# A four-layer cross-attention network on one core: earlier keys in layer 0, two score buffers in layer 3, another maximum, earlier weights and an fp32 first product in the last network, a bf16 bias in layer 2

## What is computed

```
x = x + L0_xattn(layernorm(x), ctx, ctx)      # 16 heads of 8, linear attention over 64 positions
x = x + L0_ffn(...) ; x = x + L1_xattn(...) ; x = x + L1_ffn(...) ; x = x + L2_xattn(...)
# L2_ffn: top-1 of 8 experts with a capacity, and a residual MLP beside them
a   = layer_norm(x) * attn_nw + attn_nb
res = gelu(a @ res_inter_w + res_inter_b) @ res_output_w + res_output_b
x   = x + res * coef0 + moe * coef1
# L3_xattn: rotary positions, a mask of at most 5 keys for each query
keep   = (key <= seg_id) & (key >= seg_id - 4)
scores = where(keep, q @ k.T / sqrt(8), -inf)  # 64 x 64 for each of 16 heads and 128 sequences
x = x + softmax(scores) @ v @ Wo
# L3_ffn: 16-bit activations with one scale for the whole tensor, 8-bit weights
quantize_a16(x): s = 32767 / max|x| over all tokens and features; round(x * s) / s
quantize_w8(w):  s = 127 / max|w| along one axis;                 round(w * s) / s
hidden = gelu(quantize_a16(layernorm(x)) @ quantize_w8(W_in) + b_in)
x = x + quantize_a16(hidden) @ quantize_w8(W_out) + b_out
```

## Time and profile before

| | us |
|---|---|
| median of three runs | 3071.56 |
| the three runs | 3076.02, 3067.39, 3071.56 |
| time of the profiled execution | 3070.32 |
| its span (first to last instruction) | 3068.8 |
| TensorE (PE) busy in it | 2563.7 (84%) |
| VectorE (DVE) busy | 2210.2 (72%) |
| ScalarE (ACT) busy | 1393.5 (45%) |
| GpSimd (POOL) busy | 385.9 (13%) |
| mean granted clock of TensorE | 0.927 of full |

### The profile page before, as it was taken

The page is one execution under the profiler, slowest core; times in us unless marked ns, Lnnn a source line. Parts: engine busy times, 40 slices in busy tenths (PEclk is TensorE's granted clock), DMA queues, the critical chain, the costliest instruction groups (busy, mean ns, idle before and its releaser), DMA issues. The chain is left out here.

```text
span 3068.8 us, 68519 instructions
## 1 busy us (share of the span) xinstructions
PE 2563.7 (84%) x25419; PEld 1890.9 (62%) x25454; DVE 2210.2 (72%) x5434; ACT 1393.5 (45%) x2483; POOL 385.9 (13%) x542
## 2 busy tenths in 40 slices
PE   4867769995899999999999789887979786787457
PEld 3644436663887877878876466665657454666227
DVE  6889859996567767777775388896830486888784
ACT  3548868884011111111111477764534345666364
POOL 0012210000000000000000000002321442232004
PEclk9988779997999999999999799998989898999689
DMA  3110000002113112112120000001013220000001
GB/s 92 31 67 1 0 19 16 14 13 91 76 56 111 56 61 106 56 67 99 56 80 31 21 15 15 10 2 36 26 36 110 79 66 3 0 0 0 8 0 55
DMA packets 55450, 128.94 MB, mean 42 GB/s; under 512 B 9702, under 2 KB 21350, under 8 KB 54507
## 3 DMA queue, kind: packets, MB, share of 16 engines
q1 hardware_dynamic: 47754, 106.36, 10.0%
q0 software_dynamic: 7520, 20.34, 2.2%
HBM read 109.37 MB, written 17.30 MB: 41 GB/s over the span
## 5 line engine op out<-in xcount | busy, mean ns | idle before, releaser
L1505 PE MATMUL banks<-l1f_feed,l1f_w 128*128 128x512 f32 x512 | 229.1, 598 | 1.4 <-DVE l1f_feed L1774 1.4
L1448 PE MATMUL banks<-l1f_sums,l1f_mixes 128*128 128x256 f32 x768 | 186.6, 379 | 0.0
L1774 DVE TENSOR_TENSOR l1f_feed<-l1f_aoT,l1f_rwb 128x512 f32<-128x512 f32 x256 | 158.8, 682 | 15.8 <-PE banks L1448 10.3
L1505 PEld LDWEIGHTS banks<-l1f_feed,l1f_w 128*128 128x128 f32 x512 | 95.8, 192 | 108.5 <-issue 90.0
L1448 PEld LDWEIGHTS banks<-l1f_sums,l1f_mixes 128*128 128x128 f32 x768 | 145.9, 190 | 19.9
L1448 PE MATMUL banks<-l1f_feed,l1f_mixes 128*128 128x256 f32 x512 | 135.3, 387 | 20.5 <-DVE l1f_feed L1731 20.5
L1740 DVE TENSOR_TENSOR l1f_sums<-l1f_feed 128x512 f32<-128x512 f32 x128 | 88.5, 691 | 87.8 <-PE banks L1448 84.0
L1468 PE MATMUL banks<-l1f_w,l1f_feed 128*128 128x128 f32 x1024 | 136.7, 277 | 0.0
L214 POOL COPY x<-xn 128x512 f32 (+1 forms) x16 | 9.8, 611 | 935.6 <-DVE xn L1791 935.6
L1468 PEld LDWEIGHTS banks<-l1f_w,l1f_feed 128*128 128x128 f32 x1024 | 126.2, 194 | 0.0
L1448 PEld LDWEIGHTS banks<-l1f_feed,l1f_mixes 128*128 128x128 f32 x512 | 93.1, 192 | 38.7 <-DVE l1f_feed L1731 24.5
(11 more groups left out here) (524 smaller groups left out, 7057.5 us busy)
## 6 DMA issues: line engine op xcount, KB each, us to landing
l1f_rwb<-l1f_shares SPq DMA_DIRECT2D x128, 512.0 KB, 7.0
l0a_ctxT<-in_ctxT SPq DMA_DIRECT2D x16, 256.0 KB, 2.6
l2f_sent<-l0f_zero SPq DMA_DIRECT2D x4, 1024.0 KB, 7.0
l1a_ctxT<-in_ctxT SPq DMA_DIRECT2D x16, 256.0 KB, 2.6
l2c_ctxT<-in_ctxT SPq DMA_DIRECT2D x16, 256.0 KB, 2.7
l2e_rows<-l2f_sent SPq DMA_DIRECT2D x16, 256.0 KB, 2.8
l2f_answers<-l2e_y POOLq DMA_DIRECT2D x16, 256.0 KB, 2.7
l3p_ctxT<-in_ctxT SPq DMA_DIRECT2D x16, 256.0 KB, 2.6
```

What stands on the lines that cost most here:

```text
L1448: return pe.matmul(prods[:, n, :], left, right, start=(p == 0 and first), stop=(p == PAIRS - 1), skip_group_check=True)
L1505: pe.matmul(out_bank, w[:, 1, e, :], feed[:, e % NB, :], start=(e == 0), stop=(e == E - 1)).then_inc(s.y_psum, 1)
L1774: dve.tensor_tensor(feed[:, e % NB, :], aoT[:, m, :], rwb[:, m, e, :], ALU.mult).then_inc(s.ae_ready, 1)
```

## The change

Six edits.

1. Layer-0 attention: `keys` stands first in PE's list, before `turn`.
2. Layer-3 attention: the scores have two buffers, of two whole PSUM banks each (banks 0, 1 and banks 2, 3). `score` of tile t waits for `centred` of tile t-2. The mask is two matmuls of 512 columns in place of four of 256, the scores four matmuls on 64 rows and 512 columns in place of eight on 32 rows and 256 columns. For this POOL's `kbd` has 1024 columns in place of 512, and is made before the mask. All later parts run one step later.
3. Scales: DVE takes maximum and minimum of the first 24 tiles only. For the other 40, ACT writes the absolute distance from the mean, |mean - x|, and DVE takes one maximum for every 8 tiles of these. The weights are gone from this stage.
4. Up: ACT copies the turned activations once as fp32, and PE multiplies once in fp32; DVE's `lower` is gone, `win` is fp32.
5. Layer-2 experts: SP loads the last network's weights ahead of the first rows, DVE rounds them ahead of its bias pipeline, PE and ACT turn and copy the first matrix at the stage's end. Their buffers are allocated once for layers 2 and 3.
6. Layer-2 gate: the residual bias is a bf16 matmul of 96 rows, as in layer 0; DVE prepares its three parts after the weights' arrival.

```diff
-            pipeline(pe, k.NG, [(1, turn), (2, outer), (3, project), (1, keys), (1, queries), (2, weigh), (1, values), (2, turn_o)])
+            pipeline(pe, k.NG, [(1, keys), (1, turn), (2, outer), (3, project), (1, queries), (2, weigh), (1, values), (2, turn_o)])
...
-        scores = k.banks[:, 0:4, 0:4 * S].rearrange("p a (b n) -> p a b n", n=S)
+        scores = [k.banks[:, 2 * par:2 * par + 2, :].rearrange("p a (h n) -> p (a h) n", n=S) for par in range(2)]
...
-                if mask:
-                    mask.make(pool, t, par, s.score_psum)
                 wait(pool, s.score_psum, t - 1)
                 settle(pool, k)
-                pool.tensor_tensor(kbd[:, par],
-                                   r.kT[:, bass.ds(P * t, P)].rearrange("p (b n) -> p b n", b=2).unsqueeze(2).to_broadcast([P, 2, 4, S]),
-                                   k.headmask.unsqueeze(1).unsqueeze(3).to_broadcast([P, 2, 4, S]), ALU.mult).then_inc(s.q_ready, 1)
+                pool.tensor_tensor(kbd[:, par], r.kT[:, bass.ds(P * t, P)].unsqueeze(1).to_broadcast([P, H // 2, P]),
+                                   k.headmask8.unsqueeze(2).to_broadcast([P, H // 2, P]), ALU.mult).then_inc(s.q_ready, 1)
+                mask.make(pool, t, par, s.score_psum)
...
-                wait(pe, s.centred, t)
-                    for a in range(4):
-                        pe.matmul(scores[:, a], never[:, :], rhs, start=True, stop=False, skip_group_check=True)
-                for a in range(4):
-                    lo = 32 * a
+                wait(pe, s.centred, t - 1)
+                for a in range(2):
+                    pe.matmul(ps[2 * par + a], never[:, :], rhs, start=True, stop=False, skip_group_check=True)
+                for a in range(2):
+                    rows = slice(64 * a, 64 * a + 64)
                     for b in range(2):
...
-            pipeline(pool, k.NT, [(5, copy_mv), (2, add_bias), (0, prepare)], unroll=TG)
+            pipeline(pool, k.NT, [(6, copy_mv), (2, add_bias), (0, prepare)], unroll=TG)
-            pipeline(pe, k.NT, [(1, score), (2, turn), (4, project), (3, weigh)], unroll=TG)
+            pipeline(pe, k.NT, [(2, score), (3, turn), (5, project), (4, weigh)], unroll=TG)
-            pipeline(act, k.NT, [(0, copy_q), (2, copy_v), (2, copy_pT), (1, exp)], unroll=TG)
+            pipeline(act, k.NT, [(0, copy_q), (3, copy_v), (3, copy_pT), (2, exp)], unroll=TG)
-            pipeline(dve, k.NT, [(1, centre), (3, normalise), (4, new_x)], unroll=TG)
+            pipeline(dve, k.NT, [(2, centre), (4, normalise), (5, new_x)], unroll=TG)
...
+            for t in range(FAR):
+                last = act.activation(away[:, t, :], k.x[:, OWN + t, :], ACT.Abs, bias=k.mv[:, OWN + t, 0:1], scale=-1.0)
...
-            for n in range(PIECES):
-                dve.tensor_reduce(ends[:, 0, piece], k.x[:, piece, :], AX_X, ALU.max).then_inc(s.ends_chain, 1)
-                dve.tensor_reduce(ends[:, 1, piece], k.x[:, piece, :], AX_X, ALU.min).then_inc(s.ends_chain, 1)
+            dve.tensor_reduce(ends[:, 0, :], k.x[:, 0:OWN, :], AX_X, ALU.max).then_inc(s.ends_chain, 1)
+            dve.tensor_reduce(ends[:, 1, :], k.x[:, 0:OWN, :], AX_X, ALU.min).then_inc(s.ends_chain, 1)
...
+            for n in range(FAR // PIECE):
+                dve.wait_ge(s.away_ready, n + 1)
+                dve.tensor_reduce(far[:, piece], away[:, piece, :], AX_X, ALU.max).then_inc(s.ends_chain, 1)
...
-                    pe.matmul(ps[4 + c], w.win[:, c, :], high[:, m, :], start=True, stop=False)
-                    pe.matmul(ps[4 + c], w.win[:, c, :], low[:, m, :], start=False, stop=True).then_inc(s.f_psum, 1)
+                    pe.matmul(ps[4 + c], w.win[:, c, :], hT[:, m, :], start=True, stop=True).then_inc(s.f_psum, 1)
...
-            pipeline(dve, k.NG, [(1, lower), (0, quantise), (2, largest)])
+            pipeline(dve, k.NG, [(0, quantise), (2, largest)])
...
-                pe.matmul(y_bank, k.ones[0:1, 0:P], b2[:, :], start=True, stop=False, skip_group_check=True)
+                pe.matmul(y_bank, ones[0:96, :], b2_rows[:, :].unsqueeze(1).to_broadcast([96, TG, D]), start=True, stop=False,
...
+            round_network()
             pipeline(dve, items, [(2, bias)], unroll=2 * per)
```

More of the change, by code:

```diff
@@ L2387, in _ @@
-            dve.wait_ge(s.rstd_ready, 1)
-            dve.tensor_tensor(ends[:, :, :], ends[:, :, :], both(k.rstd[:, :]), ALU.mult).then_inc(s.ends_chain, 1)
-            dve.wait_ge(s.ends_chain, 2 * PIECES + 2)
-            dve.tensor_reduce(w.most[:, 0:1], ends[:, :, :].rearrange("p a t -> p (a t)"), AX_X, ALU.max,
-                              apply_absolute_value=True).then_inc(s.most_ready, 1)
-            chain = Chain(dve, s.w_chain)
-            go = lambda ins: chain.wait(chain.did(ins))
@@ new lines, in _ @@
+            dve.wait_ge(s.ends_chain, 3 + FAR // PIECE)
+            dve.wait_ge(s.rstd_ready, 1)
+            dve.tensor_tensor(peaks[:, 0:2 * OWN].rearrange("p (a t) -> p a t", a=2), ends[:, :, :], both(k.rstd[:, 0:OWN]), ALU.mult)\
+                .then_inc(s.ends_chain, 1)
+            dve.tensor_tensor(peaks[:, 2 * OWN:], far[:, :], k.rstd[:, OWN:], ALU.mult).then_inc(s.ends_chain, 1)
+            dve.wait_ge(s.ends_chain, 5 + FAR // PIECE)
+            dve.tensor_reduce(w.most[:, 0:1], peaks[:, :], AX_X, ALU.max, apply_absolute_value=True).then_inc(s.most_ready, 1)
@@ L2415, in l3_ffn_up @@
+def l3_ffn_up(nc, k, w, hidden):
     FC = F0 // P
@@ L2459, in gelu @@
                     settle(act, k)
-                    act.activation(w.hidden[:, c, bass.ds(GT * g, GT)], ps[4 + c], ACT.Gelu,
+                    act.activation(hidden[:, c, bass.ds(GT * g, GT)], ps[4 + c], ACT.Gelu,
                                    bias=w.b_in[:, c:c + 1], scale=w.scale[:, 0, c:c + 1]).then_inc(s.f_ready, 1)
-            pipeline(act, k.NG, [(1, gelu), (0, split)])
+            pipeline(act, k.NG, [(1, gelu), (0, copy_hT)])
         @block.gpsimd
@@ L2768, in _ @@
             dve.wait_ge(s.weights, 16 * 7)
+            chain.did(dve.memset(b2_rows[:, :], 0.0))
+            go(dve.tensor_copy(b2_part[:, 0, :], b2[:, :]))
+            go(dve.tensor_tensor(b2_rest[:, :], b2[:, :], b2_part[:, 0, :], ALU.subtract))
+            go(dve.tensor_copy(b2_part[:, 1, :], b2_rest[:, :]))
+            go(dve.tensor_tensor(b2_rest[:, :], b2_rest[:, :], b2_part[:, 1, :], ALU.subtract))
+            go(dve.tensor_copy(b2_part[:, 2, :], b2_rest[:, :]))
+            for n in range(3):
+                last = dve.tensor_copy(b2_rows[32 * n:32 * n + 1, :], b2_part[32 * n:32 * n + 1, n, :])
+            last.then_inc(s.consts_ready, 1)
             def norm(g, m):
@@ L2936, in _ @@
             pipeline(pe, items, [(1, up), (0, turn), (2, down)], unroll=2 * per, behind=2 * per)
+            pe.wait_ge(s.win_ready, 1)
+            for c in range(FC):
+                last = pe.transpose(ps[1][:, P * c:P * c + P], network.in_T[:, c, :], k.ident)
+            last.then_inc(s.win_psum, 1)
         @block.scalar
```

172 lines of the change are left out of this document (85 added, 87 removed).

## The result

| | before | after |
|---|---|---|
| median, us | 3071.25 (4 runs) | 3028.86 (4 runs, 3025.30 to 3029.71) |
| ratio | | 0.9859, 95% interval 0.9847 to 0.9871 |
| profiled execution, us | 3070.32 | 3025.30 |
| its span | 3068.8 | 3023.7 |
| mean granted clock | 0.927 | 0.939 |

The account below looks back on a forecast made before the run. Barriers make each stage's saving the kernel's; layer-3 attention was bound by PE and DVE taking turns, the gate by PE. Terms -15 - 10.5 + 2.2 - 20 - 8 - 3 = -54.3 from 3070.3 gave 3016.0 us, range 3000 to 3040.

Parts of the forecast that it names:

- half of layer 3: First rival: PE bounds layer-3 attention as gaps or clock dips stay, -12 not -20; total 3029; chance 0.31 with layer-0 case.
- Layer-0 keys first: Layer-0 attention: the keys' pair runs while ACT copies, nearly closing PE's 1.23-us gap; -15 us.
- Layer-2 bias: Layer-2 gate: bf16 bias matmul takes 0.22 in place of 1.05 us, less DVE's preparation of +2.0; -10.5 us.
- Experts: Layer-2 experts: four transfers ahead of the first rows delay them, while DVE's rounding costs nothing; +2.2 us.
- Layer-3 attention: Layer-3 attention: a second score buffer removes waits between PE and DVE, a group taking 17.25 us; -20 us.
- 15.8 under 16.96: Layer-3 attention: PE's work per group of four tiles, 15.8 us, fits under DVE's own work, 16.96.
- With both gone: Layer-3 attention: without DVE's waits for PE's scores and outputs, 1.56 us a group, a group takes 16.96.
- Layer-3 attention, the clock: Layer-3 attention: clock dips go with PE's gaps, giving -20; if they stay, a group takes about 17.75, giving -12.
- slower rival: Layer-3 attention: POOL, with `kbd` doubled, becomes the bound; the term becomes +62, total 3098; chance 0.03 of slower's 0.05.
- Scales: Scales stage: DVE's reductions shrink to 24 tiles' maximum and minimum while ACT does 40 activations; -8 us.
- Up: Up stage: ACT's copy, four fp32 matmuls and the last gelu take 4.94 us a group, down from 5.27; -3 us.
- The rival with the halved clock: Up stage: at half clock the four matmuls take 7.4 us, +59, total 3073, no change; chance 0.04.

Follow-up runs that it names:

- the run with the values: The changed kernel with layer-0 attention's values product first in PE's list, keys back at their old place, experts' weight loads behind the second rows load: layer-0 attention 171.7 us.
- filler run: The changed kernel plus six bf16 matmuls of 512 columns in PE's gap in every fourth tile of layer-3 attention: stage 7.1 us shorter, kernel 3030.28 us.
- spread run: The changed kernel with DVE taking layer-3 attention's statistics one tile a step, in place of four in every fourth step: stage 291.6 us.
- two buffers without the lead: The changed kernel, but in layer-3 attention the score of tile t waits for the centring of tile t-1 again: stage 328.3 us.
- without the mask: The changed kernel with layer-3 attention's mask left out, one matmul of 64 columns replacing the two of 512: stage 300.8 us.

## Why the prediction was right in sum and wrong in its largest term

3028.86 lies in the range 3000 to 3040, 12.9 over the forecast, and closest to the rival "half of layer 3" (3029), to which I gave 0.31; the forecast case had 0.60. So the likeliest case was not the one that came. The total also had luck: 4.1 us of the difference of the two spans lie in stages that the change leaves alone, and the scales and the gate gave 3.7 more than forecast. Of the signs that I had named, the granted clock of layer 3 (0.94, not over 0.95), DVE's waits (1.48 a group, not under 0.5) and the step of the up stage (5.28, not 4.9) failed.

- **Layer-0 keys first**, -15: -14.8, as worked out. That the keys were the right thing to move rested on more than the stated reason (they need only the context); the run with the values shows that the place left behind counts as well.
- **Layer-2 bias**, -10.5: -12.1. The bias went from 1.05 to 0.22 as said, the preparation took 2.0 (2074.38 to 2076.40). The "short wait" for which I took 0.8 off did not come: a step fell by 0.96.
- **Experts**, +2.2: +1.8, inside the bounds. Rounding was hidden, as said.
- **Layer-3 attention**, -20 (bounds -27 to -8): -7.6, just outside. The step that failed is "15.8 under 16.96, PE catches up only while DVE does `new_x`". In the tile with `new_x` PE cannot catch up: it has one score of lead, and its next step waits for the exponential of a centring that DVE has not begun. PE idles there (1.80), and enters the short tiles without a reserve. "With both gone" was therefore wrong: DVE's waits for PE went from 1.56 only to 1.48 us a group, and in groups at full clock they were 1.00 before (0.29, 0.32 and 0.39, from 2783.1) and 0.95 after. The group's sum says what an engine has room for, not when.
- **Layer-3 attention, the clock.** This second part was weighed the right way round but its premise failed: the gap did not close, so the low stretches stayed, in 5 of 14 groups for 8, and cost 1.5 each for 1.0. The filler run gives this part its size, 7.1 us; the spread run gives both, 18.8. The first rival had this case but sized it too well: it gave a group 17.75 and the term -12, where the 14 groups took 18.36 each. That -7.6 lies just outside the bound of -8 says little: the same code in other runs would have given -9.5, -7.6 and -3.5.
- The Trainium skill, "TensorE: Matmul & The Clock Gate", section "HAM oscillation — how this bites in real kernels", describes a kernel that waits between short bursts in every round and pays for the lower clock in every round. The runs agree in part. Where PE's longest gap in a group was 0.4 us (filler) or 0.9 (spread), none of 14 groups had a low stretch; but with the same 1.80 in each, 9 of 14 groups kept 2.4 GHz.
- POOL's `kbd` took 1.90, as assumed (2.1), and one of PE's weight loads waited for it once in 250 us, 0.2: the slower rival had no part in it.
- **Scales**, -8: -10.1, beyond the good bound of -9.4. ACT's activations took 0.294 where I had bounded them by 0.30.
- **Up**, -3: +1.8, inside the wide bounds. The ring was mis-sized: 5.28 in most steps (5.20 in the last, shown here), in place of 4.94, at a full clock. The two ends:

```profile
2935.39 3.69 PE L2416 MATMUL banks<-l3u_hT,l3f_win 128*128 128x512 f32 x8 [1.15 <-ACT l3u_hT L2427]
2936.71 3.35 ACT L2433 ACTIVATE l3f_hidden<-banks,l3f_b_in,l3f_scale 128x512 f32 x4 [1.46 <-PE banks L2416]
...
2939.96 0.57 ACT L2427 COPY l3u_hT<-banks 128x512 f32<-128x512 f32 x1
...
2940.59 3.70 PE L2416 MATMUL banks<-l3u_hT,l3f_win 128*128 128x512 f32 x8 [1.07 <-ACT l3u_hT L2427]
```

  From the last product's end (2939.08) to the next start are 1.51 us: the rest of the gelu, 0.98, then ACT's copy, 0.57. I had 0.70 and 0.56 for them. Over the 14 later steps (73.7 us in all) that is 4.5; the first group at 1.2 GHz took 6.23 for its products and not 3.68, 2.6 more, where I had set 2 aside. The rival with the halved clock was far off: the stage was granted 0.95.

What stays open: why a gap of the same length lowers the clock in one group and not in the next; and how much of a stage's saving in a single profile is its number of low stretches.

## What to carry to other kernels

A second buffer lets the engine in front work ahead by one step. If the engine behind has one long step in four, one step of lead is not enough, and the long step's extra is paid in the short ones; spreading the same work evenly was worth about as much as the lead alone (-15.6 against -17.9), and twice the net of the two-buffer edit, whose wider form costs 10.3; DVE's busy time stayed the same. With the load even, the second buffer still gave 10.8. Compare step by step, not by the sum of a group. Before work is moved into a gap, ask what it covers at its old place: the same edit with another product of the same length lost 11 us against the kernel before, where the keys won 14.8.

## What the runs showed of the hardware that I had not expected

- Work can be added to gain time: 14 us more of matmuls in the gaps of layer-3 attention made the stage 7.1 us shorter, since TensorE kept 2.4 GHz in all 14 groups.
- The low stretches don't follow the idle time alone: with 2.2 us of PE idle in a group (after) 5 of 14 groups had one (4 to 6 in other runs of the same code), with 2.8 to 3.3 (two buffers without the lead) also 5, and before the change, at 3.5 to 4.1, 8; none had one at 1.3 (spread) and 0.8 (filler).
- The last stage, whose code no edit touched, took 74.4 to 75.6 us in nine runs, at a granted clock of 0.91 to 0.94, but 81.5 without the mask and 82.6 with the filler, at 0.94 and 0.93. So the clock isn't the cause. DVE rescales the activations there in 16 instructions of 1.23 us; in every run those during which POOL's addition of the bias (`xb`) started took 2.43 to 2.54 us, and no others did. In the nine runs that met one instruction, in the two long ones seven. From the run without the mask:

```profile
2956.30 1.23 DVE L2527 TENSOR_SCALAR l3d_f<-l3d_f 128x2048 f32<-128x2048 f32 x1 [0.47 <-ACT l3d_f L2514]
...
2961.48 2.47 DVE L2527 TENSOR_SCALAR l3d_f<-l3d_f 128x2048 f32<-128x2048 f32 x1 [1.55 <-ACT l3d_f L2514]
2961.57 1.28 POOL L206 TENSOR_TENSOR xb<-x,l3f_b_out 128x512 f32<-128x512 f32 x1
```

  These instructions took 28.6 us in all in place of 20.8, about the difference of the stages. Why the two engines fell into this rhythm in these two runs stays open. The total of a whole kernel can hide an effect of 7 us: the filler's gain in its stage doesn't show in that run's 3030.28.
